# Blocks that end without GpSimd's drain, and the second normalisation's roots made inside attention

## What is computed

```
x = x + tanh(g_xattn) * attention(layernorm(x), ctx_768, Wq, Wk, Wv, Wout, bout)   # 8 heads of 64, 77 context rows
y = layernorm(x)
scores = softmax(y @ Wg.T);  wk, idx = top_k(scores, 2)                             # 16 experts
z = sum over the two chosen experts of  wk * ((u * silu(g)) @ W2[e]),  u, g = split(y @ W1[e])
ys = (u' * silu(g')) @ Ws2,  u', g' = split(y @ Ws1)                                # shared expert
out = x + tanh(g_ffn) * (z + ys)
layernorm(x) = (x - mean) / sqrt(var + 1e-5)
```

## Time and profile before

| | us |
|---|---|
| median of 3 runs | 1073.16 |
| lowest, highest | 1066.94, 1075.34 |
| the profiled execution, whole | 1074.5 |
| its span in the trace | 1072.2 |

### The profile page before, as it was taken

How to read it: one execution, slowest core, us unless ns; L and a number is a source line. 1 busy time by engine, 2 the same in 40 slices (tenths; PEclk the granted TensorE clock), 3 DMA queues, 4 the chain that set the end, 5 groups by cost and what they waited for, 6 DMA issues and landing times. The chain is left out here.

```text
span 1072.2 us, 21198 instructions
## 1 busy us (share of the span) xinstructions
PE 948.8 (88%) x6828; PEld 873.8 (81%) x6829; DVE 797.3 (74%) x1824; ACT 471.7 (44%) x967; POOL 505.9 (47%) x635
## 2 busy tenths in 40 slices
PE   3799999999999999997799999978887877878883
PEld 3699999999999999987588888865877775877772
DVE  5699899999999998885588888881565552655552
ACT  4456555555555555542644554430333231323331
POOL 7546354544545353441235555551455553354554
PEclk9799999999999999998799999999999999999997
DMA  8213332222323221221524444456899963766650
GB/s 219 69 44 97 86 97 85 72 71 83 97 86 97 86 61 41 63 56 55 174 90 168 168 157 175 149 208 206 286 296 318 300 235 112 236 189 215 199 172 13
DMA packets 108328, 150.96 MB, mean 141 GB/s; under 512 B 21831, under 2 KB 72395, under 8 KB 108241
## 3 DMA queue, kind: packets, MB, share of 16 engines
q1 hardware_dynamic: 92880, 107.60, 33.6%
q0 software_dynamic: 15360, 42.24, 10.5%
HBM read 90.19 MB, written 65.90 MB: 146 GB/s over the span
## 5 line engine op out<-in xcount | busy, mean ns | idle before, releaser
L652 POOL TENSOR_TENSOR prob<-prob,row_sum 128x616 f32<-128x616 f32 x64 | 77.9, 1217 | 132.6 <-DVE row_sum L853 132.2
L75 PE MATMUL ps_h<-w_flat,eyT_hi 128*128 x320 | 98.3, 307 | 36.0 <-DVE eyT_lo L1610 33.0
L1491 POOL DMA_INDIRECT rows_scratch<-prow x80 | 78.7, 984 | 91.5 <-DVE prow L1628 73.1
L1491 POOL DMA_INDIRECT out<-prow x80 | 78.7, 983 | 85.5 <-DVE prow L1628 63.9
L1585 ACT ACTIVATE eyT_hi<-ps_ey 128x512 fp32r<-128x512 f32 x80 | 48.3, 604 | 139.4 <-PE ps_ey L1513 100.5
L1080 POOL DMA_INDIRECT rows_scratch<-row,slot x64 | 67.9, 1061 | 75.5 <-DVE row L1329 60.9
L1628 DVE TENSOR_TENSOR prow<-ps_z,prow 128x512 f32<-128x512 f32 x80 | 54.9, 687 | 65.0 <-PE ps_z L77 37.1
L75 PEld LDWEIGHTS ps_h<-w_flat,eyT_hi 128*128 128x128 f32 x320 | 62.0, 194 | 43.1 <-issue 43.1
L76 PE MATMUL ps_h<-w_flat,eyT_hi 128*128 x320 | 90.9, 284 | 0.0
L77 PE MATMUL ps_h<-w_flat,eyT_lo 128*128 x320 | 90.5, 283 | 0.0
L1610 DVE TENSOR_TENSOR eyT_lo<-ps_ey,eyT_hi 128x512 fp32r<-128x512 f32 x80 | 55.1, 688 | 42.3 <-ACT eyT_hi L1585 36.5
(11 more groups left out here) (267 smaller groups left out, 3410.5 us busy)
## 6 DMA issues: line engine op xcount, KB each, us to landing
prow<-rows_scratch SPq DMA_DIRECT2D x160, 258.0 KB
rows_scratch<-blank SPq DMA_DIRECT2D x34, 258.0 KB, 2.9
xT_raw<-in_xT SPq DMA_DIRECT2D x32, 256.0 KB, 4.4
x_tok<-in_x SPq DMA_DIRECT2D x32, 256.0 KB, 3.0
x_scratch<-x_tok SPq DMA_DIRECT2D x32, 256.0 KB, 3.3
row<-x_scratch SPq DMA_DIRECT2D x16, 512.0 KB, 4.0
x_ahead<-in_x SPq DMA_DIRECT2D x26, 256.0 KB, 4.3
w_raw<-in_W SPq DMA_DIRECT2D x16, 256.0 KB
```

Source lines behind the costliest of these rows:

```text
L75: nc.tensor.matmul(out, lh, rh, start=start and n == 0, stop=False)
L652: nc.gpsimd.tensor_tensor(pr, pr, row_sum[i][:, :].unsqueeze(2).broadcast_to((P, H, CK)), ALU.mult).then_inc(normed, 1)
L1491: pool.indirect_dma_start(dram, bass.IndirectOffsetOnAxis(target, 0), row[u][:, i, 0:columns], None, bounds_check=bound, oob_is_err=False) ...
```

## The change

It has four parts. **1.** The blocks of `prepare`, `attend` and `mix` are opened with `no_gpsimd_drain=True`: GpSimd runs no drain at their ends. **2.** What the drain or the old end of `attend` waited for is waited for by hand and later: SP waits for the x1 stores in `mix`, ahead of `load_rows(3)`, and for the blank rows near its end; VectorE waits for SP's word at step 1; GpSimd, at the end of `mix`, waits for its scatters (as before) and for two of its own semaphores. **3.** `rstd_steps` is gone. GpSimd makes 1/sqrt and shift of tiles 0 to 47 after group 6 and of tiles 48 to 59 after group 7, 23 steps each, with the recipe it already used for the first layernorm plus three steps for the shift; VectorE makes the last 4 tiles by the same 23 steps at the start of `mix`. `normalise` waits for that only in step 15. ScalarE takes no Sqrt; a one-column Silu at the block's start brings in its table. **4.** The `busy` matmuls are 6 instead of 10 at the start of `mix` and 11 instead of 18 at its end.

```diff
@@ -102,49 +102,26 @@
     return sb, ps, sem
-def rstd_steps(nc, v, stats, mean, rstd, var, chain, root_ready, root_done):
-
+SEED = 0x5F3759DF
+LN_STEPS = 6 + 2 + 3 * 4
+NORM_STEPS = LN_STEPS + 3
+LATE_TILES = 4
+
+
+def linked(eng, chain, before):
     step = [0]
     def link(ins):
         step[0] += 1
         ins.then_inc(chain, 1)
-        v.wait_ge(chain, step[0])
-
-    me, mo = stats[:, :, 1], stats[:, :, 4]
-
-    link(nc.vector.tensor_tensor(mean, me, mo, ALU.add))
-    link(nc.vector.tensor_scalar(mean, mean, 0.5, None, ALU.mult))
-    link(nc.vector.tensor_tensor(rstd, mean, me, ALU.subtract))
-    link(nc.vector.tensor_tensor(rstd, rstd, rstd, ALU.mult))
-    link(nc.vector.scalar_tensor_tensor(rstd, stats[:, :, 2], 1.0 / D, rstd, ALU.mult, ALU.add))
-    link(nc.vector.scalar_tensor_tensor(rstd, stats[:, :, 5], 1.0 / D, rstd, ALU.mult, ALU.add))
-    link(nc.vector.tensor_scalar(rstd, rstd, LN_EPS, None, ALU.add))
-    nc.vector.tensor_copy(var, rstd).then_inc(root_ready, 1)
-    v.wait_ge(root_done, 1)
-    link(nc.vector.reciprocal(rstd, rstd))
-
-    link(nc.vector.tensor_tensor(var, var, rstd, ALU.mult))
-    link(nc.vector.tensor_tensor(var, var, rstd, ALU.mult))
-    link(nc.vector.tensor_scalar(var, var, -0.5, 1.5, ALU.mult, ALU.add))
-    link(nc.vector.tensor_tensor(rstd, rstd, var, ALU.mult))
-
-
-SEED = 0x5F3759DF
-LN_STEPS = 6 + 2 + 3 * 4
-
-
-def rstd_on_gpsimd(nc, pool, stats, rstd, var, work, chain, before):
-
-    step = [0]
-
-    def link(ins):
-        step[0] += 1
-        ins.then_inc(chain, 1)
-        pool.wait_ge(chain, before + step[0])
-
-    g = nc.gpsimd
+        eng.wait_ge(chain, before + step[0])
+
+    return link
+
+
+def rstd_by_newton(g, link, stats, rstd, var, work):
+
     link(g.tensor_tensor(work, stats[:, :, 1], stats[:, :, 4], ALU.subtract))
     link(g.tensor_tensor(work, work, work, ALU.mult))
     link(g.tensor_scalar(work, work, 0.25, LN_EPS, ALU.mult, ALU.add))
@@ -158,6 +135,16 @@
         link(g.tensor_tensor(work, work, var, ALU.mult))
         link(g.tensor_scalar(work, work, 1.5, None, ALU.add))
         link(g.tensor_tensor(rstd, rstd, work, ALU.mult))
+
+
+def norm_of_stats(g, link, c, first, tiles, var, work):
+
+    stats = c.stats2[:, first * 6:(first + tiles) * 6].rearrange("p (t s) -> p t s", s=6)
+    rstd, shift = c.rstd2[:, first:first + tiles], c.shift2[:, first:first + tiles]
+    rstd_by_newton(g, link, stats, rstd, var, work)
+    link(g.tensor_tensor(shift, stats[:, :, 1], stats[:, :, 4], ALU.add))
+    link(g.tensor_scalar(shift, shift, -0.5, None, ALU.mult))
+    link(g.tensor_tensor(shift, shift, rstd, ALU.mult))
 def attention_tensors(nc, c, ctx):
@@ -370,7 +357,7 @@
             return w[j * DH:(j + 1) * DH, :].rearrange("p (q j) d -> p q j d", j=2)[:, :, j, :]
-        with nc.Block() as block:
+        with nc.Block(no_gpsimd_drain=True) as block:
             @block.sync
             def _(sp):
...
@@ -639,9 +629,6 @@
                 blank_rows(c.rows1)
                 blank_rows(c.rows0)
                 store(B - 1, (B - 1) % 2)
-                for par in range(2):
-                    sp.wait_ge(x1_out[par], 16 * (B // 2))
-                sp.wait_ge(c.blanked, 32)
             @block.gpsimd
             def _(pool):
...
@@ -674,6 +661,12 @@
                     if exists(g + 2):
                         pool.wait_ge(ahead_stats, 2 * GB * (g + 1))
                         rstd_of(2 * GB * (g + 2), 2 * GB, LN_STEPS * (g + 1))
+                    else:
+                        part = g - (GROUPS - 2)
+                        begin, end = 0 if part == 0 else known2, known2 if part == 0 else TILES - LATE_TILES
+                        pool.wait_ge(x1_stats, end)
+                        norm_of_stats(nc.gpsimd, linked(pool, rstd_chain, LN_STEPS * (GROUPS - 1) + NORM_STEPS * part),
+                                      c, begin, end - begin, var2[:, 0:end - begin], work2[:, 0:end - begin])
                 rstd_of(0, 4 * GB, 0)
                 groups(pool, body)
@@ -926,8 +919,8 @@
     K2 = CHOICES * E
     with ExitStack() as ctx:
         sb, ps, sem = allocator(nc, ctx)
-        mean2, var2 = sb("mean2", [P, TILES]), sb("var2", [P, TILES])
-        rstd2, shift2 = sb("rstd2", [P, TILES]), sb("shift2", [P, TILES])
+        late_var, late_work = sb("late_var", [P, LATE_TILES]), sb("late_work", [P, LATE_TILES])
+        loaded = sb("loaded", [P, 1])
         ws1 = [sb(f"ws1_{s}", [P, DC, 2 * HS], F32R) for s in ("hi", "lo")]
         ws2 = [sb(f"ws2_{s}", [P, 2, D], F32R) for s in ("hi", "lo")]
         wg_raw, wg = sb("wg_raw", [P, DC, E]), sb("wg", [P, DC, 2 * E], F32R)
...
@@ -1019,6 +1010,9 @@
                 load_rows(2)
                 load_weights(0)
                 load_weights(1)
+                for par in range(2):
+                    sp.wait_ge(c.x1_out[par], 16 * (B // 2))
+                sp.sem_inc(x1_stored, 1)
                 load_rows(3)
                 sp.wait_ge(ws_lo, 2)
                 load_rows(4)
@@ -1027,6 +1021,7 @@
                         load_rows(G + 3)
                     if G + NW < STEPS:
                         load_weights(G + NW)
+                sp.wait_ge(c.blanked, 32)
                 sp.wait_ge(tails_ready, 1)
                 blank_tails(nc, sp, nc.sync, c, c.rows1, 1, range(E), c.blanked1)
@@ -1088,6 +1083,8 @@
                         scatter(G - 1)
                 for u in range(NX):
                     pool.wait_ge(scattered[u], 64 * len(range(u, STEPS, NX)))
+                pool.wait_ge(w_lo, E)
+                pool.wait_ge(consts, 11)
             @block.tensor
             def _(pe):
@@ -1146,7 +1143,7 @@
                                  ws2[0][:, n, :], ws2[1][:, n, :]) for n in range(2)])
                         last.then_inc(o_done, 1)
-                busy(nc, c, ps_h[0], c.stats2[:, :], 10)
+                busy(nc, c, ps_h[0], c.stats2[:, :], 6)
                 transpose_y(0)
                 pe.wait_ge(wg_ready, 1)
                 score(0)
@@ -1172,7 +1169,7 @@
                                             table[0:SLOT_TILES, column:column + 1], c.ident[0:SLOT_TILES, 0:SLOT_TILES],
                                             start=True, stop=True)
                 last.then_inc(table_rows, 1)
-                busy(nc, c, ps_h[0], c.stats2[:, :], 18)
+                busy(nc, c, ps_h[0], c.stats2[:, :], 11)
             @block.scalar
             def _(act):
@@ -1205,17 +1202,17 @@
                 def normalise(G):
                     act.wait_ge(x1_in[G % NX], 16 * (G // NX + 1))
+                    if 4 * G + 4 > TILES - LATE_TILES:
+                        act.wait_ge(chain2, NORM_STEPS)
                     for i in range(4):
                         t = 4 * G + i
                         last = nc.scalar.activation(row[G % NX][:, i, D:2 * D], row[G % NX][:, i, 0:D], ACT.Identity,
-                                                    bias=shift2[:, t:t + 1], scale=rstd2[:, t:t + 1])
+                                                    bias=c.shift2[:, t:t + 1], scale=c.rstd2[:, t:t + 1])
                     last.then_inc(y_ready, 1)
+                nc.scalar.activation(loaded[:, :], c.tanh_g[:, 0:1], ACT.Silu)
                 act.wait_ge(wg_in, 16)
                 nc.scalar.activation(wg[:, :, 0:E], wg_raw[:, :, :], ACT.Copy).then_inc(wg_hi, 1)
-                act.wait_ge(root_ready, 1)
-                nc.scalar.activation(rstd2[:, :], rstd2[:, :], ACT.Sqrt).then_inc(root_done, 1)
-                act.wait_ge(ln_ready, 1)
                 normalise(0)
                 act.wait_ge(ws_in, 32)
                 nc.scalar.activation(ws1[0][:, :, :], ws1_raw, ACT.Copy).then_inc(ws_hi, 1)
@@ -1361,9 +1358,7 @@
                                            table[:, CHOICES:], ALU.mult, ALU.add).then_inc(table_ready, 1)
                     link(V.memset(c.weights_at[:, :], 0))
-                rstd_steps(nc, v, stats, mean2[:, :], rstd2[:, :], var2[:, :], chain2, root_ready, root_done)
-                V.scalar_tensor_tensor(shift2[:, :], mean2[:, :], -1.0, rstd2[:, :], ALU.mult, ALU.mult
-                                       ).then_inc(ln_ready, 1)
+                norm_of_stats(V, linked(v, chain2, 0), c, TILES - LATE_TILES, LATE_TILES, late_var[:, :], late_work[:, :])
                 v.wait_ge(wg_hi, 1)
                 V.tensor_tensor(wg[:, :, E:], wg_raw[:, :, :], f32(wg[:, :, 0:E]), ALU.subtract).then_inc(wg_ready, 1)
                 v.wait_ge(consts, 9)
@@ -1374,6 +1369,8 @@
                     if G == STEPS - 1:
                         place(G)
                         tails()
+                    if G == 1:
+                        v.wait_ge(x1_stored, 1)
                     if G >= 1:
                         multiply(G - 1, 1)
                         low_aT(G - 1, 0)
...
```

More of the change, by code:

```diff
@@ L571, in attend @@
         ps_o = [ps(f"ps_o{i}", [P, 512]) for i in range(2)]
-        x1_out = [sem(f"x1_out{i}") for i in range(2)]
+        x1_out = c.x1_out
```

(10 more changed lines are left out.)

1 line of the change is left out of this document (removed).

## The result

The changed kernel took 1060.09 us in the median of four executions (1057.06 to 1065.26), the kernel before 1072.43 (four, 1066.94 to 1075.34): ratio 0.9899, 95% interval 0.9857 to 0.9941. The profiled execution of after is the slowest of its four.

What follows compares the result with a forecast made beforehand. TensorE, at nine tenths of its time through attention and `mix`, was taken as the bound. Attention +5.3, start of `mix` -4.1 and its end -5.3 summed to -4.1: 1069.1 us from 1073.16, range 1063.5 to 1075.5.

Steps and rivals of the forecast that it cites:

- stall at batch 28: Last group of attention: TensorE waits 3.8 us for `norm(28, 0)`, delayed by GpSimd's new steps.
- meeting before `mix`: End of attention: without the drain the engines meet at 508.7 instead of 510.4, 1.7 us sooner.
- Part 1: Attention: GpSimd's 23 steps for 48 tiles stall TensorE 3.8 us, plus 1.5 at lower clock: 5.3 lost (1.8 to 8.3).
- the landing of a 256 KB load: End of `mix`, alternative bound: it lands 5.2 us after issue, so `passes` would start only 3.0 us earlier.
- Parts 2 and 3: The 12-tile steps after group 7 fit GpSimd's idle time; dropping the drain at `prepare`'s end gains nothing: 0 each.
- part 4: Attention's end and `mix`'s start: earlier meeting, then ScalarE's ws1 split waits for ws2's DMA; up to score(0) 2.8 us early.
- Part 5: Step 0 of `mix`: no Silu load, 1.3 us more; start of `mix` 4.1 early in all (2.8 to 5.7), carried to its end.
- part 6: End of `mix`: without drain and with eleven idle-time matmuls, `passes` starts 5.3 us sooner and merely keeps the gain.
- Rival B: `mix` or attention: the 6.0 us at half clock shorten by up to 3.0, or the stall costs no clock; 1066, chance 0.12.
- A: Last group of attention: GpSimd's steps fit its gap, costing 0 to 1.8 us; 1063.8, chance 0.12.
- C: End of `mix`: the drain did not hold it, so its removal is worth about 0.5 us; 1073.9, chance 0.07.
- D: Attention: a 5.3 us stall plus 3.0 to 5.0 from lower clock exceeds all gains; about 1077, chance 0.06.

Runs made afterwards that it cites:

- chain_8_first: Changed kernel with the 60 tiles' roots cut as 8 and 52 instead of 48 and 12; ratio 0.9899 to the kernel before.
- mix_drain_back: Changed kernel with GpSimd's drain put back at the end of `mix` alone, 11 idle-time matmul pairs kept; ratio 0.9987 to the kernel before.
- drain_and_dummies: Kernel before without the three drains, DMAs waited for, 6 and 11 idle-time matmul pairs, roots where they were; ratio 0.9939 to the kernel before.
- drain_only: Kernel before with only the three blocks' drains removed and DMAs waited for; ratio 1.0007 to the kernel before.
- roots_and_preload: Changed kernel with all drains and 10 and 18 idle-time matmul pairs back, leaving moved roots and early Silu load; ratio 1.0010 to the kernel before.
- third group: One of the three groups in which the experiments ran, each on one chip with the kernel before in turn.
- dummies_back: Changed kernel with 10 and 18 idle-time matmul pairs instead of 6 and 11; ratio 1.0010 to the kernel before, 7.0 us slower than the changed kernel.

## Why the prediction was off

Over all profiles the terms can be sized better than from one pair. Each number is a distance of the table above; "old" and "new" are the profiles in which that part is as before or as changed, with their count in brackets.

| term | predicted | first pair | all profiles: old, new |
|---|---|---|---|
| stall at batch 28 | +3.8 | +3.7 | 8.34 to 8.35 (6); 11.99 to 12.05 (7): +3.7 |
| lower clock behind it | +1.5 | +2.2 | 43.7 (6); 44.7 to 46.0, mean 45.4 (7): +1.7 |
| rest of attention | 0 | -2.25 | 12.6 to 16.4, mean 14.1 (6); 12.6 to 16.5, mean 14.2 (7): 0 |
| meeting before `mix` | -1.7 | -1.65 | 2.62 (2); 0.93 to 0.98 (12): -1.65 |
| `mix` to score(0) | -1.1 | -1.1 | before twice 12.2, 13.0; after three times 11.1, 11.2, 10.4: -1.7 |
| table load | -1.3 | -0.7 | 11.80 to 12.22 (5); 11.08 to 11.38 (9): -1.0 |
| score(1) to `mix`'s first scatter | none | +0.3 | table load as before: 15.5, 17.0 to 17.4, mean 16.8 (5); early: 15.5 to 15.8, 17.4, mean 16.0 (9): -0.9 |
| end of `mix` | -5.3 | -5.3 | 8.8, 9.4; 3.5, 3.9, 3.5: -5.4 |
| start of `passes` | none | -1.7 | 16.7, 18.2; 15.0, 15.2, 15.4: -2.2 |
| sum | -4.1 | -6.5 | -7.5 |

*Right.* Part 1's steps and stall held in every figure: the price by columns gave 8.7 for the 23 steps and 3.8 for the stall, measured 8.7 and 3.82, and `chain_8_first` split it into number and width as priced. The stall was not given back. The drain at `mix`'s end was the five microseconds without data (`mix_drain_back`); the landing of a 256 KB load, the other bound, did not come in. What bounds the end of `mix` now is the last of the eleven pairs (`passes` begins 0.41 behind it in three profiles of eight) or something 0.1 to 0.4 later (0.48 to 0.85 behind it in the other five), presumably the scatters' semaphores; the prediction had put the two within 0.1 of each other. The head start is carried through `mix`: first to last scatter is 180.0 to 180.4 in all profiles. Parts 2 and 3 were free. In part 4 the chain of waits is the predicted one, and ws_hi waits for its DMA in eight of the ten profiles with the moved roots; it started 9.0 behind the last `bn_stats` (519.44 - 510.43) where 8.4 was predicted (516.6 - 508.2) plus that instruction's 0.43. That the moved roots are what makes it earlier is not shown: with the old chain on VectorE it started 8.5 behind (`drain_and_dummies`).

*Mis-sized.* Part 5 gave 1.3 for the table load; it is 1.0 to 1.1. The upper bound of 1.6 more, that VectorE's slow 4-column subtraction might be rid of GpSimd's, was not reached: they meet again, 1.83 us. (The Trainium skill, "GPSIMD Engine Reference", section "Key points", names contention between GpSimd and VectorE instructions with two SBUF inputs; the trace agrees, with 1.83 for 4 columns beside GpSimd where 64 took 0.23.) The lower clock behind the stall, 1.5 in the sum, cost 1.0 to 2.2, mean 1.7.

*Missing.* The failed step is the last sentence of part 6, that `passes` has the same list and merely keeps the gain. Its start is shorter as well. In all five profiles with 18 pairs the granted clock was 0.50 for 3 to 7 us from about 6 us after the start of `passes`, where TensorE has work almost without a pause; the first scatter came after 16.7 to 18.6. With 11 pairs and no drain it was full up to there in seven of eight, and the first scatter came after 15.0 to 15.4 (in the eighth the clock fell, and it took 16.6). That is 1.7 (the first pair) to 2.2 (the means) that the sum lacks. It was in the trace before, which shows the same stretch:

```profile
745.00:748.00 3.00, 2.86 (x14) 2.86 (x15) 0.69 (x1) 0.60 (x1) 0.00 (x0) 0.50 0.95 330
```

I had looked at the clock only where a stall was added. With this term the sum is -6.6.

A smaller one is missing in the same way, in part 5's sentence that TensorE carries the head start to the end of `mix`. Behind score(1) the granted clock was 0.50 for six to seven microseconds in four of the five profiles with the Silu table loaded in step 0, and for three to four in eight of the nine with the early load; the stretch to the first scatter is 0.9 shorter in the mean, though not in the first pair. With it the sum is -7.5, which is what the three measurements give; that it fits to a tenth is luck, since single profiles of this stretch differ by up to 1.9.

Rival B named the mechanism, less time at the low clock, and is the rival that came nearest, but the stretch that it names, the 6.0 us from 523, did not shorten: the clock stayed at 0.50 for six microseconds or more behind score(0) in every profile.

*The rest of the first -12.3* is mostly sample. The span of the first pair differs by 8.8, of which the listed terms are 6.5; 1.0 more lies ahead of `norm(27, 1)` and 1.5 behind the first scatter of `passes`, both of which the prediction put at nothing. In it the stretch at the end of attention was 2.25 shorter in after, from low clock over 3 instead of 10.5 us; over 6 and 7 profiles the means differ by 0.1. I treated the profiled execution as typical, and gave the range nothing for such differences. That it was these that put four executions of each kernel at 0.9899 is likely but not shown, since only one execution of each was profiled.

*Rivals.* A fell: the steps didn't fit in the gap. C fell with `mix_drain_back`, but half of it stands: with 18 pairs left in place the drain is not what holds the end of `mix` (`drain_only`, 7.93 against 8.76). D was wrong: the stall had the middle price, and though the clock was low for six microseconds or more behind it in four profiles of seven, that cost 2.0 to 2.2 and not 3.0 to 5.0. Near it lies only this, that without the other parts the moved roots gain nothing (`roots_and_preload`, 1.001).

*Open.* Why more idle-time matmuls go with a lower clock some 6 us into `passes`, and why the table load in step 0 goes with a longer low clock behind score(1). Also, in the profiles taken outside the third group the passes from their first scatter on took 306.7 to 308.9 in the three profiles with 18 pairs and 300.4 to 307.4 in the seven with 11, whose mean is 302.9. `dummies_back` lost 7.0, and the stages up to the first scatter explain 6. In the third group no such difference stands out (249.1 and 249.6 against 249.8 and 254.3). And the stages of `drain_and_dummies`, from its one profile, add up to some 10 less than before, where it timed 6.5 less (3.7 to 9.3), and by the stages it should be 3 to 4 faster than after, which the times don't show: a sum of stages is good to about 3 us here.

## What to carry to other kernels

Put small dependent chains where their engine has a real gap before its next deadline: the same 23 steps cost nothing behind the last norm and 5.4 us one group earlier. A barrier has several holders, and taking one away pays only down to the next; drain and idle-time matmuls were worth 5.3 together and almost nothing singly. When an edit moves the start of a stage, look at the clock of that stage's first microseconds in the old trace too, and don't size a half per cent effect from four executions.
